# Top-k attention in units of 32 queries of four heads, with the choice made on exponentials, in a two-layer tower kernel

## The reference, cut to what matters

```python
scores = jnp.einsum('bhqd,bhkd->bhqk', q, k) / math.sqrt(D_HEAD)
scores = jnp.where(causal, neg_inf, scores)
vals, idx = jax.lax.top_k(scores, K_S)              # K_S = 32
masked = jnp.put_along_axis(jnp.full_like(scores, -jnp.inf), idx, vals, axis=-1, inplace=False)
attn = jax.nn.softmax(masked, axis=-1)
out = jnp.einsum('bhqk,bhkd->bhqd', attn, v)
```

## Time and profile before

| | us |
|---|---|
| median of three runs (2346.59 to 2350.22) | 2348.54 |
| the profiled execution, its own time | 2353.57 |
| its span, first to last instruction | 2351.8 |
| first `max` of the stage to last `match_replace` | 1212.1 to 2105.7 |
| DVE busy in that stretch | 883.1 of 893.6 |
| PE, ScalarE, GpSimd busy in it | 401.9, 451.6, 300.3 |

### The profile page before, as it was taken

How to read it: one execution, slowest core, us unless ns; L and a number is a source line. 1 busy time by engine, 2 the same in 40 slices (tenths; PEclk the granted TensorE clock), 3 DMA queues, 4 the chain that set the end, 5 groups by cost and what they waited for, 6 DMA issues and landing times. The chain is left out here.

```text
span 2351.8 us, 37086 instructions
## 1 busy us (share of the span) xinstructions
PE 1448.5 (62%) x8068; PEld 798.5 (34%) x8101; DVE 1645.2 (70%) x4922; ACT 953.7 (41%) x1997; POOL 463.2 (20%) x856
## 2 busy tenths in 40 slices
PE   7488889687877079991744444444444444446992
PEld 4122235344435046660422222222222222224561
DVE  4578857567765111112659999999999999986456
ACT  3266652145552022220334554554455455543330
POOL 4100002200000500005323333333333333330000
PEclk9699999889997589995765555555555555558995
DMA  5472301533314211112340000000000000001001
GB/s 164 146 243 71 113 8 53 158 84 81 74 29 211 72 36 45 45 45 80 107 124 19 19 19 20 20 19 19 19 19 19 19 19 19 19 1 46 0 0 37
DMA packets 91883, 137.62 MB, mean 59 GB/s; under 512 B 9508, under 2 KB 75948, under 8 KB 89392
## 3 DMA queue, kind: packets, MB, share of 16 engines
q1 hardware_dynamic: 88432, 127.37, 18.6%
q0 software_dynamic: 3264, 8.41, 1.1%
HBM read 82.49 MB, written 53.76 MB: 58 GB/s over the span
## 5 line engine op out<-in xcount | busy, mean ns | idle before, releaser
L1073 DVE MATCH_REPLACE8 top_left<-top_largest,top_left 128x129 f32<-128x129 f32 (+3 forms) x768 | 360.7, 477 | 0.0
L1071 DVE MAX8 top_largest<-top_left 128x8 f32<-128x129 f32 (+3 forms) x768 | 337.6, 481 | 0.8 <-DVE top_left L1073 0.8
L897 PE MATMUL top_ps_pt<-ident,top_prob 128*128 128x128 f32 x640 | 194.0, 440 | 198.8 <-POOL top_prob L1003 195.9
L978 ACT ACTIVATE top_e_left<-top_left,top_neg_max 128x129 f32<-128x129 f32 (+3 forms) x256 | 134.2, 561 | 311.5 <-DVE top_left L1073 305.9
L905 PE MATMUL top_ps_pv<-top_prob_t,top_vs 128*32 128x128 f32 x1280 | 82.9, 421 | 268.1 <-ACT top_prob_t L953 268.1
L897 PEld LDWEIGHTS top_ps_pt<-ident,top_prob 128*128 128x128 f32 x640 | 107.7, 212 | 287.3 <-POOL top_prob L1003 272.3
L1003 POOL TENSOR_TENSOR top_prob<-top_e_all,top_e_left 128x129 f32<-128x129 f32 (+3 forms) x256 | 202.5, 812 | 10.1 <-ACT top_e_left L978 3.3
L664 DVE TENSOR_REDUCE tok_rowmax<-tok_ps_s 128x1 f32<-128x512 f32 x256 | 167.0, 688 | 45.5 <-PE tok_ps_s L507 42.9
L1561 DVE TENSOR_TENSOR moe_hid<-moe_act_gate,moe_ps_h 128x512 f32<-128x512 f32 x39 | 26.8, 688 | 221.1 <-ACT moe_act_gate L1522 221.1
L905 PEld LDWEIGHTS top_ps_pv<-top_prob_t,top_vs 128*32 128x32 f32 x1280 | 50.7, 162 | 296.8 <-ACT top_prob_t L953 293.7
L664 DVE TENSOR_REDUCE rot_rowmax<-rot_ps_s 128x1 f32<-128x128 f32 (+3 forms) x256 | 115.6, 487 | 47.1 <-PE rot_ps_s L510 43.2
(11 more groups left out here) (327 smaller groups left out, 3102.3 us busy)
## 6 DMA issues: line engine op xcount, KB each, us to landing
moe_w<-in_moe_w SPq DMA_DIRECT2D x3, 4096.0 KB, 24.0
moe_xs<-zeros SPq DMA_DIRECT2D x1, 5120.0 KB, 20.1
last_xs<-zeros SPq DMA_DIRECT2D x1, 5120.0 KB, 33.0
moe_rows<-moe_xs SPq DMA_DIRECT2D x40, 128.0 KB
moe_ys<-moe_y SPq DMA_DIRECT2D x38, 128.0 KB, 1.7
v_rows<-tok_va SPq DMA_DIRECT2D x4, 1024.0 KB, 5.2
tok_vs<-v_rows SPq DMA_DIRECT2D x16, 256.0 KB
v_rows<-rot_va SPq DMA_DIRECT2D x4, 1024.0 KB, 5.0
```

The costliest lines, as they stand in the source:

```text
L897: mm = pe.transpose(ps_t[:, i, ch * P:ch * P + P], prob[:, qt % 2, u % HG, 1 + ch * P:1 + ch * P + P], c.ident[:, :])
L978: act.activation(e_left[:, i, 0:w], left[:, j, 0:w], ACT.Exp, bias=neg_max[:, j:j + 1]).then_inc(left_ok, 1)
L1071: ins = dve.max(largest[:, at, j // 2, :], src)
L1073: ins = dve.match_replace(left[:, at, 0:w], largest[:, at, j // 2, :], src, TAKEN)
```

## The change

A unit becomes 32 consecutive queries of all four heads of a group, again 128 rows: row 32h + r is query r of head h. A step has 16 such units and the keys grow by 32 with each: 33, 65, ... 513 columns. The score products are made head by head into 32 rows each. The 32 by 32 triangle on the diagonal is masked in the same product: contraction rows 96 to 127 of `qs` and `ks` hold an identity and a mask, written once by DVE.

DVE reads the row maximum straight from PSUM; ScalarE makes the exponential of the whole row once, and of the eight largest; DVE strikes out on the exponentials, with zeros; GpSimd subtracts what is left. The copy out of PSUM and the second exponential are gone. Values are stored by position with the class position first (`c.vp`), so the class key needs no path of its own; a 513th column is transposed and multiplied apart (`ps_tail`, `tail_t`). Rows of the transposed probabilities are kept by chunk and head. GpSimd clears the end of the last chunk. Reciprocals and scaling go image by image, the scaling on GpSimd. All loops over steps are written out.

```diff
+            if by_position:
+                dve.wait_ge(vc_ones, 2)
+                dve.tensor_copy(vc[:, :, 0:HD], c.vcls[:, :].rearrange("b (h d) -> b h d", d=HD)).then_inc(vc_ok, 1)
...
+            if by_position:
+                pool.memset(vc[:, :, :], 0.0).then_inc(vc_ones, 1)
+                pool.wait_ge(vc_ones, 1)
+                pool.memset(vc[:, :, HD:HD + 1], 1.0).then_inc(vc_ones, 1)
...
+        def keys(U):
+            return 1 + QS * (U % per_step + 1)
...
+            def scores(U):
...
+                if U >= SLOTS:
+                    pe.wait_ge(e_ok, U - SLOTS + 1)
+                for h in range(HG):
...
+                    pe.matmul(ps[lanes, base:base + own - first], q[0:PARTS * HD, h, mine],
+                              k[0:PARTS * HD, h, first:own], start=True, stop=True)
+                    mm = pe.matmul(ps[lanes, base + own - first:base + own - first + QS], q[:, h, mine],
+                                   k[:, h, own:own + QS], start=True, stop=True)
+                mm.then_inc(s_mm, 1)
...
+            for U in range(4, units + 6, 2):
+                if U < units:
+                    scores(U)
+                if U >= 6:
+                    turn(U - 6)
+                    turn(U - 5)
+                if U + 1 < units:
+                    scores(U + 1)
+                if U >= 6 and U % 4 == 0:
+                    values((U - 6) // 4)
+                elif U >= 10:
+                    turn_back((U - 8) // 4)
...
+            def expo(U):
+                if U >= KEPT:
+                    act.wait_ge(t_mm, U - KEPT + 1)
+                act.wait_ge(neg_ok, U + 1)
+                act.activation(e[:, U % KEPT, 0:keys(U)], row(U), ACT.Exp, bias=neg_max[:, U % 4:U % 4 + 1]
+                               ).then_inc(e_ok, 1)
+                act.activation(e8[:, U % 4, :], raw8[:, U % 4, :], ACT.Exp, bias=neg_max[:, U % 4:U % 4 + 1]
+                               ).then_inc(e8_ok, 1)
...
+            for U in range(2, units + 4, 2):
+                if U < units:
+                    expo(U)
+                    expo(U + 1)
+                if U >= 4:
+                    turned(U - 4)
+                    turned(U - 3)
+                if U >= 6 and U % 4 == 2:
+                    rows((U - 4) // 4)
+                elif U >= 8:
+                    returned((U - 8) // 4)
...
+            for U in range(2, units, 2):
+                if U >= 4:
+                    subtract(U - 4)
+                    subtract(U - 3)
+                negate(U)
+                negate(U + 1)
+                if U + 2 < units:
+                    pad(U + 2)
+                    pad(U + 3)
+                if U % (units // B) == 8 and U > 8:
+                    scale(U // (units // B) - 1)
...
+            for U in range(0, units, 2):
+                pair = (U, U + 1)
+                for u in pair:
+                    take_first(u)
+                for u in pair:
+                    find(u, 1)
+                if U + 2 < units:
+                    largest(U + 2)
+                    largest(U + 3)
+                for step in (2, 4):
+                    for u in pair:
+                        take(u, step)
+                    for u in pair:
+                        find(u, step + 1)
+                for u in pair:
+                    take(u, 6)
```

More of the change, by code:

```diff
@@ L196, in project @@
     turns = 2 if rope else 0
+    by_position = cls and not rope
     with c.stage() as st:
@@ L764, in _, with load_by_position @@
             finish(B - 1, G - 1)
+def load_by_position(sp, c, b, g, v, loaded):
+    heads = slice(g * P, g * P + P)
+    sp.dma_start(v[:, 0:NQ, :], c.vp[b, 0:S, heads].rearrange("(n p) w -> p n w", p=P)).then_inc(loaded, 16)
+    sp.dma_start(v[0:1, NQ:, :], c.vp[b:b + 1, S:S + 1, heads]).then_inc(loaded, 16)
 def attend_top(c, tag):
     nc = c.nc
-    units = NQ * HG
-    pairs = units // 2
-    rounds = K_TOP // 8
-    ops = 2 * rounds
+    QS = STRIP
+    per_step = S // QS
+    units = B * G * per_step
+    blocks = units // 4
     WIDE = S + 1
+    SLOTS = 4
+    KEPT = 8
     with c.stage() as st:
@@ L912, in use @@
-            def use(b, g, k):
-                turn_pair(b, g, k)
-                if 2 * k % HG == HG - 2:
-                    values(b, g, 2 * k // HG)
-            def step(b, g, before, more):
-                for k, last in with_before(b, g, before):
-                    ahead(score_pair, b, g, k, more)
-                    if last:
-                        use(*last)
-            for b in range(B):
-                mm = pe.matmul(ps_s[:, b // 2, b % 2 * S:b % 2 * S + D], c.pick_cls[:, b, :], c.vcls[:, :],
-                               start=True, stop=True)
@@ new lines, in turn_back @@
+            def turn_back(n):
+                pe.wait_ge(pv_out, n + 1)
+                pe.transpose(ps_back, pv_rows[:, :], c.ident[:, :]).then_inc(bt_mm, 1)
+            pe.wait_ge(masks_ok, 2 + 2 * HG)
+            for U in range(4):
+                scores(U)
+            for U in range(4, units + 6, 2):
+                if U < units:
+                    scores(U)
+                if U >= 6:
[7 more added lines that the diff above has]
+                    turn_back((U - 8) // 4)
@@ new lines, in pad, with subtract @@
+            def pad(U):
+                if U >= KEPT:
+                    pool.wait_ge(t_mm, U - KEPT + 1)
+                if keys(U) < P * chunks(U):
+                    pool.memset(e[:, U % KEPT, keys(U):P * chunks(U)], 0.0).then_inc(pad_ok, 1)
+                else:
+                    pool.sem_inc(pad_ok, 1)
+            def subtract(U):
+                w = keys(U)
+                pool.wait_ge(left_ok, U + 1)
+                pool.tensor_tensor(e[:, U % KEPT, 0:w], e[:, U % KEPT, 0:w], left[:, U % 4, 0:w], ALU.subtract
+                                   ).then_inc(prob_ok, 1)
@@ new lines, in _ @@
+            negate(1)
+            for U in range(2, units, 2):
+                if U >= 4:
+                    subtract(U - 4)
[7 more added lines that the diff above has]
+                    scale(U // (units // B) - 1)
+            for U in range(units - 4, units):
+                subtract(U)
@@ L1049, in _ @@
+            scale(B - 1)
         @block.vector
         def _(dve):
[L1051 to L1074 removed]
@@ new lines, in take, with denominators @@
+            def take(U, step):
+                w = keys(U)
+                dve.wait_ge(pick, U // 2 * 12 + 2 * (step - 1) + 1 + U % 2)
+                ins = dve.match_replace(left[:, U % 4, 0:w], next8[:, U % 2, step // 2 - 1, :], left[:, U % 4, 0:w], 0.0)
+                ins.then_inc(left_ok if step == 6 else pick, 1)
+            def denominators(b):
+                dve.wait_ge(back_ok, NQ * G * (b + 1))
+                tiles = slice(b * NQ, b * NQ + NQ)
+                dve.reciprocal(rden[:, tiles, :], ctx[:, tiles, :, HD]).then_inc(den_ok, 1)
@@ new lines, in _ @@
+            dve.tensor_copy(c.ctx[0:B, NT, :], c.vcls[:, :]).then_inc(masks_ok, 1)
+            largest(0)
+            largest(1)
+            for U in range(0, units, 2):
[14 more added lines that the diff above has]
+                    take(u, 6)
+                if U % (units // B) == 6 and U > 6:
+                    denominators(U // (units // B) - 1)
```

393 lines of the change are left out of this document (158 added, 235 removed).

## The result

The changed kernel takes 2252.29 us (median, 2251.66 to 2252.83), the kernel before 2349.38 us beside it (2346.59 to 2352.29); the ratio is 0.9586, with a 95% interval of 0.9574 to 0.9599. The prediction was 2264, with a range of 2235 to 2308: the sign and the range held, and the gain is 97 us where 85 were forecast. The profiled execution took 2252.28 us, with a span of 2250.5.

The account below looks back on a forecast made before the run. VectorE was taken to bound the stage: 776 + 2 + 9.2 + 24 = 811 us against 893.6, -82.6, with +2.5 for start and projection and -4.7 at the end: -85, median 2264 us, range 2235 to 2308.

Parts of the forecast that it names:

- Widths: VectorE's eight operations per unit: mean 273 columns instead of 321, 776 us by the line, 102 less.
- the rival of a floor at narrow widths: VectorE's narrow operations cost as much as at 129 columns: +19 us, 2283, inside the main range; no separate chance.
- Gaps: VectorE's 15.6 us of gaps in the stage: 6.4 go with the loop, 9.2 stay.
- Where a step ends: VectorE waits after the widest pair, at the next narrow pairs: 1.6 us at each of 15 boundaries, 24 us.
- The sign set for it: VectorE's idle time before replacements of 97 and 161 columns and the PSUM maximum behind them, some 24 us.
- the two rivals that stood on them: Step boundaries cost nothing (2240 us, chance 0.15), or VectorE starves there at 5 us each (2315 us, 0.18).
- TensorE: Scores, transposes, values and turning back take 3.8 us a pair of units, against VectorE's 6.1.
- The time for a change between full and 32-column products: On TensorE, four changes a pair of units at about 0.1 us each, 0.4 a pair, hidden.
- Start: Stage start: fewer loads awaited but a longer chain to VectorE's first pair, +1.5 us; projection's wait for clearing, +1.
- End: From last replacement to last scaling: 10.7 us instead of 15.4, so -4.7.
- free boundaries: TensorE and ScalarE run far enough ahead that step boundaries cost nothing: 2240 us, chance 0.15.
- TensorE as the bound: Score products do not overlap, 7.0 us a pair: about 2349 us, or 2400 with mode changes; chance 0.07.

Follow-up runs that it names:

- the first experiment: The kernel before, with the loops over steps and images of the top-k attention written out on all engines, nothing else: 2339.64 us, ratio 0.9951.
- the version with the rows later: The changed kernel with ScalarE's copy of the value products one turn later, behind the next pair's exponentials: 2236.06 us, ratio 0.9518.
- the one-group run: The changed kernel with every score product issued twice, the first pass's four heads writing the same 32 rows: 2249.91 us, ratio 0.9571.
- the wide version: The changed kernel with seven of a unit's eight VectorE operations run over whole chunks of 128 columns: 2319.56 us, ratio 0.987.

## Why the prediction came out as it did

The bound, the reason and the sign were right; that the parts at the boundary added up to the measured price was in part luck. The profiled execution is 101.3 us shorter where -85 had been summed. By the prediction's steps:

- **Widths: right.** -102 was forecast. 16 steps of 48.57 us are 777.1, against 878 by the line: -100.9, the narrow pairs included. The maximum from PSUM costs what the one from SBUF does (682 ns and 677 for 513 columns), and the rival of a floor at narrow widths is ruled out by rounds 0.61 us apart.
- **Gaps: the step that was mis-sized.** "The 6.4 us go with the loop. I keep the other 9.2." What is left is 803.4 - 777.1 - 15 x 1.57 = 2.7 us, of which 0.8 are the stage's first wait (counted under the start below) and most of the other 1.9 are three reciprocals of 0.55 us. Part of the 9.2 had belonged to the loop too: the first experiment takes 10.2 us out of the kernel before, not 6.4. I had counted as the loop's only the wait whose releaser reads "issue", and not the short waits beside it. This is 7.3 us of the miss. (That the rest of it, 5.4 us in that experiment, went as well, no run tells apart.)
- **Where a step ends: the sum was right, two of its parts were not.** 1.6 us were forecast and 1.57 measured. At the exponentials of 97 and 129 columns 0.4 was forecast and 0.50 is what the version with the rows later keeps. At the scores 0.4 was forecast and nothing came, because a unit's scores take 0.37 us there and not 0.8. Behind the value products 0.8 was forecast; the wait for the exponential of 161 columns is 0.78, but its neighbour of 193 columns had been left out, and moving the copy gave back 1.07. The errors cancelled, which is luck. The sign set for it, some 24 us of idle time in the rows, did not come: they list 14.6, since the second operand of a pair shows no idle time. The bounds of 0 and 5 us each, and with them the two rivals that stood on them, are out.
- **TensorE: over-sized, without effect.** A pair was put at 3.8 us; it is 409.7 / 128 = 3.2. Doubling the scores costs nothing, and the one-group run shows why they are cheap. The time for a change between full and 32-column products was sized about right. The last transpose at the boundary shown, and the score product at 1513.14 behind it:

```profile
1512.79 0.42 PE L912 MATMUL top_ps_pt<-ident,top_e 128*128 128x128 f32 x1
```

These starts are 0.35 us apart, where the transposes are 0.21 apart: 0.14 more, for 0.1 forecast, and hidden. The Trainium skill, TensorEngine Tiling (Array Packing), Key Properties, has different tiles execute in parallel, and with that the runs agree (four products in 0.18 us in four groups, 0.16 to 0.19 for each in one). It also has a change of tiling mode drain TensorE; the 0.14 us at this place agree with that.

- **Start: sign wrong, small.** +1.5 was forecast; the way to the first maximum is 1.6 shorter and the first wait gives 0.8 back, -0.8. About 0.85 us of it are the loads (the value rows), 0.7 the way from the first score to the first maximum, which had not been in the sum; the table load lay under the loads and was no part of the chain. For the projection +1 was forecast. From its memset to the stage's first load it is 58.36 us after (1137.02 to 1195.38) and 58.12 before, +0.2; but with the loops written out it is 56.81 in the kernel before, and the other changed kernels have 57.6 to 59.0, so the forecast is neither borne out nor refuted.
- **End: right.** -4.7 was forecast, -5.1 measured.
- **The rest.** The stages that the change does not touch were 4.6 us shorter than in the profiled execution of before, which stood 5 us above its median. I had taken off these 5 for the median, so they are no miss. Against the medians the miss is 12 us: 7.3 from the gaps, 3.1 from start and projection, 0.9 from the widths (-102 and +2 for the narrow pairs were forecast, -100.9 came), 0.8 from boundaries and end.

The rivals: free boundaries did not come. By an estimate, 15 x 1.57 us off the measured 2252.3, they would give about 2229 in this kernel; the version at 2236 has gone two thirds of that way, with 0.50 of the 1.57 us left. TensorE as the bound is ruled out by the doubled products.

## What to carry to other kernels

Where one engine runs a long series of the same operation, fit a line through its spacing at two widths and count widths: here the sum over 33 to 513 columns came within 0.2%. Price a new boundary between long and short pieces by writing out the chain in order of each engine's own queue, and afterwards read its cost from the period of a repeated instruction and not from the list of waits: 0.97 us a boundary were listed and 1.57 were paid, and in the wide version nothing was listed and 0.31 paid. Then look what stands ahead of the late instruction in its own engine's order and waits for somebody else; moving that one copy was worth 16 us, while pulling one of two late producers ahead was worth nothing.

## What was not expected of the hardware

TensorE's granted clock rose when TensorE was given more of the same small products. In the stage it was 0.50 with 410 us busy of 803, that is 1.2 GHz, and 0.51 with the products doubled in four groups (462 us busy). In the run with the first pass in one group it was 0.64, with 533 us busy: part of the time at the upper level of 2.4 GHz and the rest at the lower one. The page's row of that run (beside the earlier trace rows):

```profile
PEclk9699998969999659999586666667665675669995
```

The stage took as long, 802.4 us for 803.4, but its steps were less alike, 49.2 to 50.6 us for 50.1 to 50.6: TensorE is in the chain at the boundaries. VectorE's chain of that run has 1.4 us of waits for scores that after the change it does not have; what the higher clock gave back against that is not told apart.

VectorE and GpSimd scaling at the same time took 0.59 and 0.81 us a product, where alone they had taken 0.34 (5.45 us for 16) and 0.59 (2.35 us for four).
